# Routed experts of a two-layer transformer on one core: where the third matrix' two parts are made in a tile's order, and what TensorE waits for and reads ahead of each product

## What is computed

```python
logits = xf @ gate_W.T                       # 4096 tokens, 8 experts
pi = _sinkhorn(-logits)
_, top_idx = jax.lax.top_k(pi, TOP_K)        # two experts for each token
g = jnp.einsum('nd,efd->enf', xf, W_gate)    # D = 256, F = 1024
u = jnp.einsum('nd,efd->enf', xf, W_up)
y = jnp.einsum('enf,edf->end', jax.nn.silu(g) * u, W_down)
for k in range(TOP_K):
    out = out + y[top_idx[:, k], n_ar] * pi[:, k:k + 1]
```

## Time and profile before

| | us |
|---|---|
| median of 3 runs | 2107.75 (2105.91 to 2108.53) |
| the profiled execution | 2104.67 |
| its span, first to last instruction | 2102.4 |
| first and last matmul of the experts' tile loop | 720.9 and 1385.7 |

### The profile page before, as it was taken

How to read it: one execution, slowest core, us unless ns; L and a number is a source line. 1 busy time by engine, 2 the same in 40 slices (tenths; PEclk the granted TensorE clock), 3 DMA queues, 4 the chain that set the end, 5 groups by cost and what they waited for, 6 DMA issues and landing times. The chain is left out here.

```text
span 2102.4 us, 37210 instructions
## 1 busy us (share of the span) xinstructions
PE 1893.3 (90%) x11671; PEld 1072.3 (51%) x11671; DVE 1332.9 (63%) x2223; ACT 1386.7 (66%) x1586; POOL 706.3 (34%) x696
## 2 busy tenths in 40 slices
PE   6989999999956589999999999949899999999898
PEld 5822333333332478888878888847522222222255
DVE  4511135345667756565565656437599999999967
ACT  5689999999933223233233333227699999999934
POOL 2000111111110212222222122111188888898922
PEclk9999999999965599999999999979899999999999
DMA  6744334434210474555555555459935344364012
GB/s 200 250 100 71 46 76 91 90 71 90 54 42 0 160 246 160 205 181 194 184 187 182 180 196 172 158 200 347 254 60 127 61 76 113 46 159 61 24 68 72
DMA packets 133132, 276.06 MB, mean 131 GB/s; under 512 B 18732, under 2 KB 69166, under 8 KB 132104
## 3 DMA queue, kind: packets, MB, share of 16 engines
q1 hardware_dynamic: 119256, 231.86, 40.4%
q10 hardware_dynamic: 6848, 22.94, 3.4%
q0 software_dynamic: 6816, 18.62, 2.6%
HBM read 365.58 MB, written 96.21 MB: 220 GB/s over the span
## 5 line engine op out<-in xcount | busy, mean ns | idle before, releaser
L1326 PE MATMUL psum<-A_qa,A_ka 50*128 50x512 f32 x2048 | 408.2, 467 | 23.2 <-DVE A_qa L1413 6.2
L1326 PEld LDWEIGHTS psum<-A_qa,A_ka 50*128 50x128 f32 x2048 | 176.6, 185 | 471.6 <-DVE A1f_probs L1423 243.6
L2714 PE MATMUL psum<-e_w_high,e_xT 128*128 x1136 | 377.2, 404 | 28.0 <-issue 28.0
L1547 POOL TENSOR_TENSOR A1f_probs<-A1f_probs,A1f_bias 128x512 f32<-128x512 f32 x256 | 327.5, 1291 | 82.5 <-ACT A1f_probs L1378 82.0
L1423 DVE SCALAR_TENSOR_TENSOR A1f_probs<-psum,A1f_bias 128x1024 f32<-128x1024 f32 x256 | 311.7, 1218 | 23.7 <-PE psum L1326 20.2
L1378 ACT ACTIVATE A0f_probs<-psum 128x1024 f32<-128x1024 f32 x256 | 316.3, 1236 | 0.0
L1366 ACT ACTIVATE A0f_probs<-psum 128x1024 f32<-128x1024 f32 x256 | 314.0, 1226 | 2.5 <-PE psum L1326 2.4
L1345 PE MATMUL psum<-A1f_probs,v 128*32 128x512 f32 x2048 | 274.2, 606 | 17.5 <-POOL A1f_probs L1547 16.4
L1370 ACT ACTIVATE A1f_probs<-A1f_probs 128x1024 f32<-128x1024 f32 x256 | 273.9, 1070 | 4.8 <-DVE A1f_probs L1423 3.9
L1345 PE MATMUL psum<-A0f_probs,v 128*32 128x512 f32 x2048 | 273.5, 606 | 0.0
L1378 ACT ACTIVATE A1f_probs<-psum 128x1024 f32<-128x1024 f32 x256 | 263.7, 1030 | 0.0
(11 more groups left out here) (308 smaller groups left out, 2534.1 us busy)
## 6 DMA issues: line engine op xcount, KB each, us to landing
e_w_raw<-in_experts ACTq DMA_DIRECT2D x67, 2048.0 KB
e_w_raw<-in_experts ACTq DMA_DIRECT2D x67, 1024.0 KB
hidden<-e_squares SPq DMA_DIRECT2D x69, 512.0 KB, 3.3
e_turned<-hidden SPq DMA_DIRECT2D x276, 128.0 KB, 2.7
qk_parts<-L_part SPq DMA_DIRECT2D x64, 512.0 KB, 4.4
A_qa<-qk_parts SPq DMA_DIRECT2D x192, 128.0 KB, 4.4
A_ka<-qk_parts SPq DMA_DIRECT2D x192, 128.0 KB, 6.6
om<-results SPq DMA_DIRECT2D x16, 512.0 KB, 6.9
```

The lines of the kernel that those rows point to most:

```text
L1326: mm = e.matmul(ps[:, side * HALF:(side + 1) * HALF], self.qk.ka[rows, s, pair, kt * P:(kt + 1) * P].bitcast(FP32R), self.qk.qa[rows, s, p ...
L1547: e.tensor_tensor(fourth, fourth, self.bias_of(*w[1:], slice(self.FOURTH, GH)).rearrange("p h q -> p (h q)"), ALU.mult).then_inc(self.mult ...
L2714: mm = e.matmul(out, left[part].bitcast(FP32R), moving.bitcast(FP32R), start=start and i == 0, stop=stop and i == 2)
```

## The change

VectorE makes the low part of a new down matrix at the end of a tile, behind the gate's, and no more between `rest_of_hidden` and `split_rows`. ScalarE makes its high part one tile later than before (in tile j for the matrix of tile j - 3) and ahead of `move_y`; the fetch of down for tile j - 4 follows it, then that of gate and up, then `move_y`. ScalarE loads its three registers right behind silu, ahead of the waits. TensorE loads both registers ahead of the wait; the wait ahead of the gate product asks for the gate part of tile j - 2, and the one for the up part of tile j - 2 stands ahead of the up product. The two functions that count follow the new order.

```diff
--- before.py
+++ after.py
@@ -2359,8 +2359,8 @@
         order = []
         for k in range(1, MOE_TILES):
             order += [("second", k)] * (k < self.REST) + [("up", k)] * (k < self.LAST)
-            order += [("down", k - self.LAG + 1)] * (k >= self.LAG) + [("second", k + 1)] * (k + 1 == self.REST)
-        order += [("down", self.LAST - 1)]
+            order += [("down", k - self.LAG)] * (k > self.LAG) + [("second", k + 1)] * (k + 1 == self.REST)
+        order += [("down", self.LAST - 2), ("down", self.LAST - 1)]
         return order.index((kind, j)) + 1
 
     def low_value(self, kind, j):
@@ -2369,8 +2369,8 @@
         order = []
         for k in range(1, MOE_TILES):
             order += [("second", k)] * (k < self.REST) + [("rest", 3)] * (k == 3)
-            order += [("down", k - self.LAG)] * (k > self.LAG) + [("rest", 2)] * (k == 2)
-            order += [("up", k - 1)] * (k > 1) + [("gate", k)] * (k < self.LAST) + [("rest", 1)] * (k == 1)
+            order += [("rest", 2)] * (k == 2) + [("up", k - 1)] * (k > 1) + [("gate", k)] * (k < self.LAST)
+            order += [("down", k - self.LAG)] * (k > self.LAG) + [("rest", 1)] * (k == 1)
         order += [("down", self.LAST - 2), ("down", self.LAST - 1)]
         return order.index((kind, j)) + 1
 
@@ -2532,8 +2532,18 @@
                 e.wait_ge(self.squared, j)
             e.activation(self.hid[:, :], self.GU[:, 0, :], ACT.Silu).then_inc(self.silu, 1)
             if 1 <= j < self.LAST:
+                self.flag(e, flags, IS_NEW, j)
+            if 1 <= j - 1 <= self.LAST_FETCH:
+                self.flag(e, flags, OTHER_BUFFER, j - 1)
+                self.flag(e, flags, FOURTH, j - 1)
+            if 1 <= j < self.LAST:
                 e.wait_ge(self.upped, j)
                 high_part(j, "up", 0, DOWN_AT)
+            if j > self.LAG:
+                high_part(j - self.LAG, "down", DOWN_AT, WIDE)
+            if j > self.LAG + 1:
+                e.wait_ge(self.low_ready, self.low_value("down", j - self.LAG - 1))
+                self.fetch_next(e, flags, j - self.LAG - 1, (DOWN_AT, WIDE), self.second_in)
             if 1 <= j - 1 <= self.LAST_FETCH:
                 e.wait_ge(self.low_ready, self.low_value("up", j - 1))
                 self.fetch_next(e, flags, j - 1, (0, DOWN_AT), self.weights_in)
@@ -2542,12 +2552,11 @@
                     split_hidden(i)
             if j >= self.LAG:
                 move_y(j - self.LAG)
-                high_part(j - self.LAG + 1, "down", DOWN_AT, WIDE)
-            if j > self.LAG:
-                e.wait_ge(self.low_ready, self.low_value("down", j - self.LAG))
-                self.fetch_next(e, flags, j - self.LAG, (DOWN_AT, WIDE), self.second_in)
             if j + 1 == self.REST:
                 high_second(self.REST)
+        e.wait_ge(self.low_ready, self.low_value("down", self.LAST_FETCH))
+        self.fetch_next(e, flags, self.LAST_FETCH, (DOWN_AT, WIDE), self.second_in)
+        high_part(self.LAST - 2, "down", DOWN_AT, WIDE)
         split_hidden(self.LAST)
         for j in range(MOE_TILES - self.LAG, MOE_TILES):
             move_y(j)
@@ -2660,8 +2669,6 @@
                 rest_of_hidden(j - self.LAG)
             if j == 3:
                 low_rest(DOWN_AT, WIDE)
-            if j > self.LAG:
-                low_part(j - self.LAG, "down", DOWN_AT, WIDE)
             if j + 1 < MOE_TILES:
                 split_rows(j + 1)
             if j == 2:
@@ -2677,6 +2684,8 @@
                 square(j)
             if 1 <= j < self.LAST:
                 low_part(j, "gate", 0, DC * F)
+            if j > self.LAG:
+                low_part(j - self.LAG, "down", DOWN_AT, WIDE)
             if j == 1:
                 low_rest(0, DC * F)
             if j >= 8:
@@ -2699,8 +2708,10 @@
             return new[j]
 
         def wait_for_weights(j):
+            buffer_of(j)
+            is_new(j)
             if j > self.REST:
-                e.wait_ge(self.low_ready, self.low_value("up", j - 2))
+                e.wait_ge(self.low_ready, self.low_value("gate" if j > self.REST + 1 else "up", j - 2))
             else:
                 with e.If(is_new(j) > 0):
                     e.wait_ge(self.low_ready, self.low_value("second", 1) if j == 1 else self.low_value("rest", 2))
@@ -2769,6 +2780,8 @@
             up_product(j, 0)
             if j > self.BY_PE:
                 turn_hidden(j - 1)
+            if j > self.REST + 1:
+                e.wait_ge(self.low_ready, self.low_value("up", j - 2))
             up_product(j, 1)
             if j >= self.LAG:
                 down(j - self.LAG)
```

## The result

| | before | after |
|---|---|---|
| median, us | 2108.14 (2105.91 to 2110.16) | 2081.66 (2079.90 to 2083.55) |
| ratio to before, 95% interval | | 0.9875 [0.9858, 0.9892] |
| span of the profiled execution | 2102.4 | 2080.2 |
| experts' tiles 8 to 69 (61 tiles), by TensorE's transposes | 562.6 | 534.5 |
| tiles 0 to 8 | 73.95 | 76.79 |

The change brings 26 us. The forecast was 40.5, with 2067 for the time; 2081.66 lies inside its range, near the upper end, in the part that it had given to its rival "half comes back". Nearly all of the gain is where it was put, between tiles 8 and 69 (28.1 us in these two profiles); the first eight tiles are 2.8 us longer, and the 0.9 and 2.2 us longer ahead of and behind the tiles 0 to 69 make the rest of the spans' difference.

A forecast was written before the change was run, and what follows sets the result against it. TensorE was taken to lose 40.2 us in tiles 5 to 69, mostly at two late waits per expert. -40.2, -0.7 at the start and +0.4 at the end gave -40.5, so 2067 us, range 2063 to 2084.

The forecast's parts named there:

- half comes back: Rival: late multiply or hidden-tile reload keeps 1 to 3 us per expert, 17.5 us remain, about 2085; chance 0.17.
- forecast's own case: Experts' loop: the stalls of all seven expert groups go, giving 2063 to 2072 us; chance 0.70.
- What bounds the kernel: TensorE in tiles 5 to 69: 40.2 us lost by tile starts, mainly two stalls per expert, at tiles m + 2 and m + 4.
- TensorE's wait: Gate product of tile m + 2: asking for the earlier gate part, with loads ahead, removes each group's first stall, about 2 us.
- Down's low part: VectorE, tile m + 3: moved to the tile's end with 1.4 us slack, it removes second stall, short waits and clock falls.
- The clock's share: Behind four of the seven second stalls the granted clock falls, losing 1.68 us each, 6.7 in all.
- What is late next there: Up product of tile m + 2 needs multiply(m + 1); slack 0.9 us, 0.5 for the experts of 20 and 27.
- The size of the delay: ScalarE's two extra loads delay the high part 1.06 us; VectorE's 0.5 us idle absorbs some, leaving 0.6 for multiply.
- As they are in 50 ordinary tiles: TensorE's register loads are hidden under the down product's matmuls wherever the wait is no longer late.
- Start: Tile 3: loads ahead of the wait save about 1 us, the clock may take half back; -0.7 us.
- End: Loop's end: ScalarE's drain and empty fetch ahead of the last splits cost nothing to 0.8 us; +0.4 taken.
- The slower rival: ScalarE's longer path delays the hidden tile beyond 2.1 us slack in every tile, +4 to +56 us; chance 0.05.

The follow-up runs named there:

- run with both moves of loads: Changed kernel with ScalarE's two fetch loads moved behind up's high part and TensorE's two loads ahead of the down product: 2068.72 us, ratio 0.9802.
- second experiment: Kernel before, with only TensorE's waits split by matrix (gate part, then up part) and its loads left behind the wait: 2090.55 us, ratio 0.9908.
- first: Kernel before, with only TensorE's two register loads moved ahead of the wait for low parts: 2097.0 us, ratio 0.9948.
- the order alone: Changed kernel with both TensorE edits undone, leaving only the new order on VectorE and ScalarE: 2099.04 us, ratio 0.9950.

## Why the prediction was right, and which steps fell short

**The time: in the range, but not as forecast.** The forecast's own case was 2063 to 2072, at 0.70. 2081.66 lies in the middle of the rival "half of it comes back as other waits" (2072 to 2089, at 0.17); the range holds it because its high end took in most of that rival. Some 12.7 us of the 40 came back as other waits in tiles 8 to 69. A wait of the down product for the hidden tile by ScalarE's path was named among the signs of being wrong, and it is there.

**What bounds the kernel: right.** The loss in tiles 5 to 69 was put at 40.2 us by tile starts, not at 33.0 by idle rows. The run with both moves of loads takes all of it away: 521.75 us for tiles 8 to 69 against 562.6, 40.9 less, and its median of 2068.7 lies within 2 us of the forecast. (The kernel before had 2111.73 beside it; by the ratio of 0.9802 the forecast's own 2107.75 gives 2066.) Idle rows understate a stall, here as there: in m + 2 of the changed kernel the bracket says 0.66 where the starts have 0.91 (1.04 - 0.13).

**TensorE's wait: right in its mechanism.** Asking for gate's part alone takes the first stall (second experiment), reading the registers early takes most of it too (first).

**Down's low part: right.** The second stall, the short waits behind it and the clock's falls there went with the order alone (which then had five falls behind its longer first stall). The clock's share was taken from one profile: 6.7 us for four falls there, 3.3 in the second with two.

**"What is late next there": the step that failed.** It looked at multiply(m + 1) and the up product of m + 2 and gave it 0.9 us of slack. But on VectorE the hidden tile's low part stands between gate's low part and up's, and the down product that needs it comes already in tile m + 1. Its slack can be had from the trace of before: it was 1.0 us (1069.73 + 1.23 = 1070.96, needed at 1066.29 + 5.66 = 1071.95). The prediction weighed the hidden tile only in an ordinary tile (2.1 us) and on its way through DRAM, never behind the late low part. With the delay of 0.6 us that it had put, this path would still have been in time; the term below had to be wrong as well.

**The size of the delay: 0.6 us put, 1.46 measured.** The 1.06 for ScalarE's loads was right (1.03). But the 0.5 us of idle time on VectorE that was to absorb half was no slack: it is VectorE's own register load, which comes behind the wait for the high part. From the high part's end to the low part's start it is 1.25 us now (1057.83 + 3.63 = 1061.46 to 1062.71), where it had been 0.82, and the 0.43 between them are the load's 744 ns for 315. No term stood for that. An estimate of its weight: with the load as short as before, the hidden tile's low part would end 5.5 us into tiles 38, 45, 53 and 61, ahead of the 5.66 at which it is wanted, and only 0.1 to 0.3 us behind it in tiles 12, 21 and 28.

**"As they are in 50 ordinary tiles": too simple.** That the loads are hidden under the down product holds as long as TensorE's queue reaches them well before the array is done. Behind the late hidden tile it doesn't, and m + 2 loses 0.8 to 0.95 us. The Trainium skill (TensorE: Matmul & The Clock Gate, section Step-by-step: what each phase is for) describes instructions queued at the array ahead of their turn, so that issue is hidden; the trace agrees for tile 36 and shows the other half for tile 38: there the queue had stood at a wait, and behind 24 small matmuls its second load comes only 0.35 us before the array is done, not 1.2.

Together: m + 1 4.7 us, m + 2 6.1, others 1.9, which is the 12.7 between 534.46 and 521.75. The rival "half of it comes back as other waits" had the size (17.5 us put), but looked for it at other places (multiply, reload).

**Start: -0.7 put, 1.4 gained in tile 3 itself, nothing visible in tiles 0 to 8.** Tile 3, where the loads now stand ahead of the wait, took 16.04 and 15.17 before and 13.84 and 14.33 after. The other runs bear it out: all ten profiles with the loads ahead of the wait have 13.84 to 14.50 (mean 14.2), the four with them behind it 15.01 to 16.46 (mean 15.7). But the stall at tiles 5 to 7, which is absent in one profile of the kernel before and 4.5 us in the other, is larger than that. **End: +0.4 put;** from tile 69 to the loop's last matmul it is about 0.2 longer.

**The slower rival** had no support: ordinary tiles are at 8.56 as before. It named the right resource, though. ScalarE's loads behind silu are what costs; with five instead of three, 9 us more are lost, at two tiles a group and not in every tile.

## What to carry to other kernels

When a stall goes, list for every product downstream when its input was ready and when it was needed in the old trace, the tile in which the delayed engine works first; the smallest slack decides, and "idle by issue" ahead of an instruction is often its own register load and no slack. Read registers ahead of the longest stretch of work on their engine, not just ahead of one wait. A fix that removes 2 us a group leaves the group's next limit at tenths of a microsecond; two moved pairs of loads were worth another 12.7 us here. And a load moved in time may fall on other traffic: its length in the old trace is not a given.

## What the hardware showed

- A register load costs TensorE's queue 0.30 us, and with the two instructions behind it about 0.6 to 0.7 from one load to the next in the rows above; two of them and a branch are free in a tile whose queue runs 1 us ahead, and cost 0.9 us in one where it had to wait.
- One register load on VectorE took 297 to 315 ns in 63 cases and 701 to 823 ns in 35, all of the latter at the onset of a burst of DMA traffic (1061.5 us above).
- The releaser that the profile names need not be the cause. "`<-DVEq L2649`" in the changed kernel disappeared when TensorE's own loads were moved, with VectorE untouched.
- Behind the same stall the clock falls in some executions and not in others (tiles 15 and 56 of the two profiles of the kernel before, 1.6 us each).
